# Inverse transform along the height: full-array matmuls replaced by matmuls on the 64x64 quarters

## The reference, cut to what matters

```python
x_ft = jnp.fft.rfft2(x, norm='ortho')
out = jnp.einsum('bixy,ioxy->boxy', x_ft[:, :, :M1, :M2], w.astype(x_ft.dtype))   # M1 = M2 = 20
out_ft = out_ft.at[:, :, :M1, :M2].set(out)                                       # the rest is zero
x1 = jnp.fft.irfft2(out_ft, s=(H, W), norm='ortho')
x  = gelu(x1 + einsum('bchw,oc->bohw', x, cw) + cb)
```

## Time and profile before

| | |
|---|---|
| median of 3 runs | 6577.88 us |
| profiled execution | 6565.23 us, of which span 6563.4 us |
| PE busy | 5753.6 us, 88% of the span |
| DVE, ACT, POOL busy | 44%, 41%, 17% |
| granted TensorE clock, mean | 0.94 |

### The profile page before, as it was taken

The page is one execution under the profiler, slowest core; times in us unless marked ns, Lnnn a source line. Parts: engine busy times, 40 slices in busy tenths (PEclk is TensorE's granted clock), DMA queues, the critical chain, the costliest instruction groups (busy, mean ns, idle before and its releaser), DMA issues. The chain is left out here.

```text
span 6563.4 us, 235714 instructions
## 1 busy us (share of the span) xinstructions
PE 5753.6 (88%) x100766; PEld 4399.3 (67%) x100766; DVE 2862.4 (44%) x4334; ACT 2661.3 (41%) x4948; POOL 1096.6 (17%) x1048
## 2 busy tenths in 40 slices
PE   5999999998998999999999998998995777877777
PEld 4887788688868876887788688868873434243333
DVE  2443444344434443443444344434442737465563
ACT  2334433433353334334433533353333737354553
POOL 3220322022222212220322032222210000000000
PEclk9999999999999999999999999999997888888887
DMA  2101101111101111101111110101101000000000
GB/s 32 13 13 14 18 13 13 15 17 16 20 9 23 13 13 19 13 13 13 18 13 13 15 17 13 23 7 21 15 3 21 1 7 1 0 7 1 4 1 4
DMA packets 442544, 82.73 MB, mean 13 GB/s; under 512 B 437305, under 2 KB 437577, under 8 KB 441417
## 3 DMA queue, kind: packets, MB, share of 16 engines
q1 hardware_dynamic: 441544, 67.56, 8.2%
HBM read 63.31 MB, written 4.23 MB: 10 GB/s over the span
## 5 line engine op out<-in xcount | busy, mean ns | idle before, releaser
L217 POOL COPY x_T<-x_X 128x512 f32<-128x512 f32 x1024 | 1067.4, 1101 | 3736.3 <-ACTq L718 3565.8
L713 ACT ACTIVATE x_X<-ga 128x512 f32<-128x512 f32 x1280 | 751.2, 597 | 899.7 <-PE ga L433 693.9
L591 DVE COPY x_X<-ev 128x512 f32<-128x512 f32 x640 | 442.6, 692 | 1281.7 <-PE ev L451 1217.7
L433 PEld LDWEIGHTS ga<-pw_rhs,x_X 64*64 64x64 f32 x32768 | 608.1, 135 | 303.1 <-issue 300.0
L681 ACT ACTIVATE V<-ga 104x512 f32<-104x512 f32 x416 | 248.4, 597 | 1043.7 <-PE ga L401 1043.7
L401 PE MATMUL ev<-inv_h,D 104*104 104x128 f32 x4864 | 617.8, 276 | 36.9 <-DVE D L591 35.9
L433 PE MATMUL ga<-pw_rhs,x_X 64*64 64x64 f32 x32768 | 606.0, 218 | 27.3 <-issue 24.2
L591 DVE COPY V<-ev 104x512 f32<-104x512 f32 x608 | 420.5, 692 | 471.0 <-PE ev L401 471.0
L401 PEld LDWEIGHTS ev<-inv_h,D 104*104 104x104 f32 x4864 | 560.0, 171 | 72.8 <-DVE D L591 27.0
L463 PEld LDWEIGHTS ev<-dft_consts,x_T 128*64 128x64 f32 x16384 | 575.0, 137 | 42.9 <-issue 42.9
L463 PE MATMUL ev<-dft_consts,x_T 128*64 128x80 f32 x16384 | 594.9, 233 | 6.2 <-POOL x_T L217 5.6
(11 more groups left out here) (192 smaller groups left out, 7674.3 us busy)
## 6 DMA issues: line engine op xcount, KB each, us to landing
mix_w<-in_sw SPq DMA_DIRECT2D x128, 400.0 KB, 8.2
coords<-in_coords SPq DMA_DIRECT2D x64, 96.0 KB, 2.1
maps<-Y SPq DMA_DIRECT2D x128, 16.0 KB
raw<-maps SPq DMA_DIRECT2D x8, 256.0 KB, 3.5
out<-out_t SPq DMA_DIRECT2D x8, 256.0 KB, 3.1
w<-in_w SPq DMA_DIRECT2D x3, 512.0 KB, 6.6
fc_rhs<-in_fc_w SPq DMA_DIRECT2D x32, 0.4 KB
dft_consts<-in_dft SPq DMA_DIRECT2D x1, 336.0 KB
```

The lines of the kernel that those rows point to most:

```text
L217: pool.tensor_copy(x_T[:, :, H * bc + h0:H * bc + h0 + 16].rearrange("p c (s n) -> p c s n", n=2), blocks.rearrange("p (s a n c) -> p a c ...
L433: last = pe.matmul(ps[HALF * bp:HALF * bp + HALF, HALF * s:HALF * s + HALF], x_X[r:r + HALF, g, col:col + HALF], pw_rhs[r:r + HALF, :], st ...
L591: dve.tensor_copy(dst, src).then_inc(ev_taken, 1)
L713: x_new = act.activation(blocks.rearrange("p (s a n) -> p s a n", s=8, a=2)[:, :, bc, :], ga[n % N_GA][:, :].rearrange("p (s n) -> p s n", ...
```

## The change

`inverse_h` on TensorE works on the four 64x64 quarters of the array instead of on all of it. A step now covers 8 columns and two banks: the bank `pair[bp]` holds image pair half bp. For each column and each (bp, bc) there is one matmul with stationary `D[r:r+40, column, 64 bc : 64 bc + m]` (m is 64 for bc = 0 and 40 for bc = 1, so the output rows keep their places) and moving `inv_h[r:r+40, r:r+64]`, 64 columns. That holds for every group and every phase. A `passed()` stands behind each of the two bank waits. VectorE and ScalarE copy the same number of elements as before, from a bank laid out as 8 columns x 64 heights instead of 4 x 128.

```diff
-                    for i in range(INV_T):
-                        ps = ga_tile() if shared and i % 2 else ev_tile()
-                        for s in range(4):
-                            last = pe.matmul(ps[0:HALF + KR, P * s:P * s + P], D[0:HALF + KR, 4 * i + s, 0:HALF + KR],
-                                             inv_h[0:HALF + KR, :], start=True, stop=True)
-                        last.then_inc(ga_ready if shared and i % 2 else ev_ready, 1)
+                    for i in range(INV_T // 2):
+                        pair = [ev_tile()]
+                        passed()
+                        pair.append(ga_tile() if shared else ev_tile())
+                        passed()
+                        for s in range(8):
+                            for bp, ps in enumerate(pair):
+                                r = HALF * bp
+                                for bc, m in enumerate((HALF, KR)):
+                                    last = pe.matmul(ps[HALF * bc:HALF * bc + m, HALF * s:HALF * s + HALF],
+                                                     D[r:r + KR, 8 * i + s, HALF * bc:HALF * bc + m],
+                                                     inv_h[r:r + KR, r:r + HALF], start=True, stop=True)
+                                if s == 7:
+                                    last.then_inc(ga_ready if shared and bp else ev_ready, 1)
@@ VectorE, inverse_h
-                        take(V[0:HALF + KR, :, 4 * i:4 * i + 4],
-                             ev_tile()[0:HALF + KR, :].rearrange("p (c n) -> p n c", n=P))
+                        n0, c0 = HALF * (i % 2), 8 * (i // 2)
+                        take(V[0:HALF + KR, n0:n0 + HALF, c0:c0 + 8],
+                             ev_tile()[0:HALF + KR, :].rearrange("p (c n) -> p n c", n=HALF))
@@ ScalarE, inverse_h
-                        act.activation(V[0:HALF + KR, :, 4 * i:4 * i + 4],
-                                       ga[m % N_GA][0:HALF + KR, :].rearrange("p (c n) -> p n c", n=P), ACT.Copy)\
+                        act.activation(V[0:HALF + KR, HALF:P, 4 * i - 4:4 * i + 4],
+                                       ga[m % N_GA][0:HALF + KR, :].rearrange("p (c n) -> p n c", n=HALF), ACT.Copy)\
```

## The result

The changed kernel takes 6843.58 us (6838.87 to 6852.97, 4 runs) against 6576.84 us before on the same chip: ratio 1.0406, 95% interval 1.0388 to 1.0425. It is 267 us slower; 6410 us had been forecast, with a chance of 0.09 for slower. The profiled execution took 6839.56 us, its span is 6837.8 us and the mean granted clock 0.881 instead of 0.94.

A forecast was written before the change was run, and what follows sets the result against it. TensorE's stream was taken to bound the Fourier part: 161 us gained in inverse_h, less 5 in first groups, plus 12 in L433, is 168 us, so 6577.88 - 168 = 6410 us; 8-in-10 range 6270 to 6515 us.

The forecast's parts named there:

- TensorE's stream bounds the Fourier part: Fourier part: TensorE, busy 88% of the span, sets the time; what inverse_h gives up is gained unless its stream is late.
- as today: Lateness between turn_d and inverse_h, where TensorE waits for VectorE's copies of D: expected to stay unchanged.
- the bound of 7 us: Last phase, VectorE emptying two banks per step: no extra cost expected, at most 0.3 us x 24 groups = 7 us.
- Array pace of 3.76 us: inverse_h: 256 quarter records at 14.7 ns each take 3.76 us by array time, instead of 7.16 us.
- Queue instructions, 1.2 us: inverse_h: register computations and no-ops ahead of each of four steps show 0.3 us each, 1.2 us, between nothing and 2.0.
- Instruction fetch, 1.0 us: inverse_h: one block boundary, sometimes part of a second, is late by 1.1 us; taken as 1.0 us, giving 5.9 us.
- the gain of 161 us: All 128 inverses: inverse_h falling from 7.16 to 5.9 us each gains 161 us.
- rival C: inverse_h paced wholly by instruction fetch, 7.2 us, stops behind it growing: about 6578 us or up to 60 better; chance 0.07.
- Elsewhere, no net change to speak of: Rest of TensorE's stream: block boundaries fall on other instructions, stops in L433 may move or grow; 12 us gain taken.
- +1.0 us a group: Stops elsewhere in TensorE's stream: the worse end of the forecast's bounds, 1.0 us more a group; the other end 0.5 less.
- -12 us: Stops in L433: half of today's 24.2 us taken to go, 12 us or 0.1 us a group.
- rival D: Clock drops to 0.50 for 6.8 us after each inverse_h, costing 2.1 us net x 128: 6850 us; chance 0.09.

The follow-up runs named there:

- e10: Kernel before, with inverse_h on quarters of 64 rows only in groups 1 to 3 of the last phase; 6578.08 us, ratio 0.9982.
- e2: Changed kernel with inverse_h doing 16 of its 32 columns, 128 moving columns per quarter matmul, half the instructions (result not the transform's); 6343.58 us, ratio 0.9635.
- e5: Changed kernel with inverse_h steps alternating between quarters with 64 rows and the whole array, same result, 160 records; 6507.24 us, ratio 0.9888.
- e7: Changed kernel with 64 no-ops ahead of the loops on TensorE's queue, so all later instructions stand 64 places later; 6805.65 us, one run.
- e1: Changed kernel with quarter matmuls of 64 rows and 64 columns of D, the added ones holding zeros; 6714.89 us, ratio 1.0199.
- e8: e5 with one no-op behind both bank waits of a step instead of two, where banks come from both rings; 6478.55 us, ratio 0.9835.
- e9: e5 with 40 rows instead of 64 in the quarter matmuls, same result; 6554.18 us, ratio 0.9950.
- e3: Changed kernel with inverse_h on two row halves, matmuls of 40 rows and 104 columns of D, 128 records instead of 256; 6958.61 us, ratio 1.0572.

## Why the prediction was wrong, point by point

**TensorE's stream bounds the Fourier part: right.** No engine took its place, and nearly everything that changed is on "issue" or at the low clock; the waits on V at L425, on Y and on S kept their sizes. Two waits on VectorE grew by 27 us together:

```profile
PE ev L407 <- DVE D L599: 53.9, 56, 1.3
...
PE ev L407 <- DVE V L599: 9.1, 24, 0.4
```

The first was 35.9 us and had been put at "as today"; the second, in the last phase, is new and a little over the bound of 7 us. e10 has such waits as well.

**Array pace of 3.76 us: right as a floor.** Between stops the sets of four follow each other in 0.058 us, as in L433; e2 shows 3.5 us plus at most 0.7. The Trainium skill (TensorEngine Tiling (Array Packing), section Theoretical Speedup) gives up to 2 for dimensions of at most 64. The array did that between stops (0.058 us for what took 0.109), and the kernel got slower.

**Queue instructions, 1.2 us: too much, but small.** e2 bounds them, with all that is between steps, at 0.7 us for four steps; e5 has 0.9.

**Instruction fetch, 1.0 us: the step that failed first.** The mechanism was right (e2, e7) and its size was off by three. The words were: "So of the two boundaries in it one, sometimes part of a second, is late by 3.5 - 2.4 = 1.1 us". At full clock the inverse took 7.33 us (e1), which less 3.76 and 0.7 leaves 2.9 us of stops. The forecast had one boundary late, by 1.1 us; the middle inverses of e1 have 1.7 long stops on average, and those in the rows shown are 1.4 us long. The stream between two boundaries was sized about right: in e1 PE is busy 2.43 of the 3.80 us, against the 2.4 us that I took. Two other things were wrong. Blocks come not every 3.5 us but, as the restarts 322.60, 326.83, 330.72 of the changed kernel and 315.38, 319.18 of e1 show, every 3.8 to 4.2 us; I had taken the one clean pair in mixing. Between the two restarts in groups 1 and 3 of all middle phases it is 4.0 us on average in the changed kernel (3.8 to 4.4, 5th to 95th percentile) and 3.9 and 4.2 us in e1. And the block in waiting is used up before the inverse begins: the last boundary of forward_w falls 19 records (in group 3, 25) ahead of it, and only there is the next block asked for. In e1 that boundary passes at 311.15, the next packet starts at 312.78, and the stream has used up the block at 313.76, 2.6 us after it entered it; there it stops until 315.38. In group 3 the boundary in forward_w is never late, and the stop before record 99 is there all the same. This term alone turns the gain of 161 us into nothing (948 us in all inverses of e1 against 955). That was rival C, priced at no gain and given 0.07. The Trainium skill (Runtime: NRT & Kernel Launch, section Instruction fetch mechanics) holds that crossing a block is mostly hidden. Here it is so in L451 (no idle time in the changed kernel) and is not wherever records of quarters follow each other for a whole block: 1.4 us at a boundary in e1. The same page of the Trainium skill also says that the instruction buffer of TensorE holds several such blocks; the packets, each starting only after a restart, show no more than one ahead.

**Elsewhere, no net change to speak of: wrong.** With the clock kept up in the middle groups (e1) L425 and L433 cost 60 us more, forward_h 37, mixing 22, forward_w 12, turn_d 10. Of the 60 us, 33 stand behind the first inverses, where the clock is at 0.50 for 103 us. Forward_h has 22 us of new stops on "issue" in e1. That the rest is boundaries that fall on other instructions is argued, not shown. The stops inside L433 did shrink, from 24.2 to 20.6 us in e1 and to 7.0 in the changed kernel, as forecast; the loss is elsewhere. I had bounded it at +1.0 us a group, 128 us; it was about that, and I had taken -12 us.

**The clock, rival D, 0.09: it came, and by luck at its price.** The prediction itself had the clock inside the middle groups at 1.00; it is at 0.50 in 68 of 72. Priced at 6.8 us of 0.50 a group and 6850 us; measured 6843.58. But the agreement is of two errors: the inverse gained nothing where I had credited 1.3 us, and the low clock cost less than 2.1 + 1.3 us a group (in the middle groups 0.6 us of inverse_h and 1.0 us of forward_h, by the change against e1), since TensorE stands still in part of it. By the difference of e1 and the change the low clock that 64 rows take away costs 1.0406 - 1.0199 = 2.1%, some 136 us, most of it in the middle groups; the stops, what they bring elsewhere and the low clock that is left cost the other 2.0%. I had argued against D that the inverse is denser than mixing, by columns in time. It is (3.76 us of columns in 5.9 was the forecast, 3.76 in 7.3 the outcome), but each quarter matmul works with 40 of 64 rows, and half of them with 40 of 64 columns, and that is what e1 changed with nothing else.

## What to carry to other kernels

Splitting a matmul over the array's quarters multiplies instructions, not only rate: count the records between two block boundaries (128 with their weight loads) and compare their time with the 3.8 to 4.2 us that a block takes here. Mix dense and slow matmuls so that no block is shorter than that; e5 and e8 do, and turned a loss of 4.1% into gains of 1.1 and 1.65%. Where a stage has pauses, keep as many rows and columns of the array at work as there are, zeros included: 64 rows instead of 40 cost nothing (6.28 us a middle inverse in e5 and in e9) and were worth 2.1% here.

## What the runs showed of the hardware that was not expected

- Instruction blocks for TensorE arrive every 3.8 to 4.2 us when it waits for them (315.38 and 319.18 in e1; 322.60, 326.83 and 330.72 in the changed kernel), and stops fall before the same records in nearly every middle phase, 31 or 32 records earlier when 64 instructions are put in front. A stop ends some 1.4 us after the transfer of an instruction packet has ended.
- The granted clock fell with 40 rows where it did not with 64. The same number and order of instructions met 0.50, in the inverse or behind it in forward_h, in 68 of 72 middle inverses with 40 rows and in 8 of 72 with 64 rows whose added rows are zeros; with 40 rows and few long stops (16 of 72 inverses have one in e2, 9 of 72 in e9) in none.
- PE busy is no sign of it: in e3 it was 7.12 of 7.12 us and the clock fell in every inverse.
- Two row halves with 104 weights each take 0.0915 us for a pair of matmul records of 64 columns, against 0.058 us for a set of four on the quarters; that the weights set this pace fits, and is not shown.
